# A mixture-of-experts decoder layer: row numbers of a block's last transfer staged and put in place one block later, and the next expert's first weight splits issued ahead of the block counts

## The chip, the cores and the metric

One core of one Trainium2 chip runs the whole program. The metric is device time in microseconds (us), the median of three runs.

## What is computed

The reference is a decoder layer on x of shape (4, 1024, 1024) in float32: causal self-attention with 16 heads, an attention against a context of width 512, and a feed-forward part with 64 experts. Each is added to x. Only the last part, cut to what matters, is touched:

```python
logits = x @ gate_weight.T                       # 4096 tokens, 64 experts
top_val, top_idx = lax.top_k(softmax(logits), 8) # top_val divided by its sum
rerouted = mapping[top_idx]                      # some experts stand in for others
...
gate, up = split(ragged_dot(x[tok], gate_up_proj.T, group_sizes))   # 1024 -> 2 x 384
y = ragged_dot(silu(gate) * up, down_proj.T, group_sizes)           # 384 -> 1024
out = zeros_like(x).at[tok].add(y * w[:, None])
```

How many tokens an expert has is known only at run time.

## The kernel before

The program has four stages: self-attention, mixing with the context, routing, and the experts, from about 3720 us to the end at 7836 us. Only the function `experts` changes.

**Precision.** A float32 product is made of three float32r products: each operand is split into a rounded part (`_hi`) and a rest (`_lo`). ScalarE (ACT in the profile) writes the rounded part with an activation, VectorE (DVE) subtracts it to get the rest, and TensorE (PE) multiplies hi*hi, lo*hi and hi*lo (L1946 to L1948).

**The loop.** All engines run the same loop, `for_experts` (before: L1805 to L1815), over 64 experts. For each expert a `super_block` handles 4 x 128 tokens with the expert's weights. If the expert has more tokens, a counted number of `tail_block`s follows, 64 tokens each, with the same weights. How many there are is the difference of two counts, which each engine reads from SBUF into its registers (`tails_before`, a TENSOR_LOAD, L1803). In `for_experts`, a function `first` may run at the head of an expert, ahead of these two reads; before the change only VectorE has one (`first_weights`, L2333).

**Weights.** An expert has 9 chunks of 512 KB: 0 to 5 for gate and up, 6 to 8 for down. SyncE (SP) loads them into a ring of three slots of `raw_w`; chunk c + 3 is loaded once the rest of chunk c has been made. ScalarE's `split(c)` (L2123) writes `gu_hi` from `raw_w` (L2134), in two halves; VectorE's `rest_of(e, c)` writes `gu_lo` (L2331). TensorE's first layer of an expert waits for the first half of chunk 0's rest.

**Blocks and their last transfer.** A block's results are added to `out` in HBM by indirect transfers that GpSimd (POOL) issues: three for the first three groups of a super block (`send_super`), and for its last group, as for a tail block's only one, two transfers of 64 rows each from `y_last` (`send_last`, L1901, then `send_second`, L1908). These two belong to block n but are issued in block n + 1: ScalarE's `finish_last(n)` (L2114) scales TensorE's result into `y_last` with `w_last`, and the two transfers take their row numbers from `scatter_l` and `scatter_m`. Both transfers raise `yl_sent`; the second waits for the first to land.

The row numbers for the next last transfer may be written into `scatter_l` and `scatter_m` only when the two transfers of this block have landed. VectorE waits for that and copies them: in the middle of a super block (L2378 to L2381), and as the last thing in a tail block (L2424 to L2427).

**The end of a tail block.** TensorE's order is: first layer for the third of the hidden width (f = 2), transpose of f = 1, transpose of the next rows (`turn_tail`, L1982), second layer f = 0, transpose of f = 2, second layer f = 1 and f = 2 (L1954, L1955). ScalarE and VectorE split f = 2's transposed activations (`split_h(2)`, L2195; `rest_of_h(2)`, L2405), which f = 2's second layer waits for, and then the rows that `turn_tail` transposed (`split_tail`, L2104; `rest_of_tail`, L2298).

Of the kernel before, what the change touches and what calls it, by code (L numbers as in the profile page):

```python
# [20 lines left out]
I32 = mybir.dt.int32  # L21
# [5 lines left out]
P = 128  # L27
# [8 lines left out]
FB = F // P  # L36
# [4 lines left out]
START = 1  # L41
# [39 lines left out]
def stand_alone(eng, passed):  # L81


    eng.sem_inc(passed, 1)
# [1634 lines left out]
def experts(nc, const, logits, lo16, hi16, starts, w_gu, w_down, rows, out):  # L1719
# [14 lines left out]
    with ExitStack() as scope:  # L1734
# [29 lines left out]
        scatter_l = m.sb("scatter_l", [P, 1], I32)  # L1764
        scatter_m = m.sb("scatter_m", [T, 1], I32)
        table = m.sb("table", [P, 1 + TAILS + SUP * (E + AHEAD) + LISTED], I32)
        own = m.sb("own", [P, 1])
# [15 lines left out]
        set_up = m.sem("set_up")  # L1783
        mask_ok, list_a, list_ps, list_id, found_ok, list_ok = (
            m.sem(n) for n in ("mask_ok", "list_a", "list_ps", "list_id", "found_ok", "list_ok"))

# [303 lines left out]
        def _(act):  # L2090
# [27 lines left out]
            for i in range(SUP):  # L2118
                split_super(0, i)

            def super_block(e, t0, t1):
                def split(c):

                    act.wait_ge(raw_in[c % RING], START + (e * 3 + c // RING) * 16 + 16)
                    if c < GUC:
                        act.wait_ge(up_ok, START + e * FB)
                        act.wait_ge(tgu_ok, START + t0 * FB)
                        dst = gu_hi[:, c // 2, c % 2 * HALF:(c % 2 + 1) * HALF]
                    else:
                        act.wait_ge(yl_ps, START + (e + t0) * 2 + 2)  # L2130
                        dst = dn_hi[:, c - GUC, :]
                    for q in range(2):
                        a = slice(q * BANK, (q + 1) * BANK)
                        act.activation(dst[:, a], raw_w[:, c % RING, a], ACT.Copy).then_inc(hi_ok, 1)  # L2134

                def silu_of(f):
# [20 lines left out]

                split(0)
                split(1)
                finish_last(e + t0)  # L2160
                split(2)
                split(3)
                silu_of(0)
                split_h(0)
                split(4)
                split(5)
                silu_of(1)
                split_h(1)
                for c in range(GUC, CHUNKS):
                    split(c)  # L2170
                split_tail(e + t0, t0)
# [7 lines left out]
            def tail_block(e, t):  # L2179
# [24 lines left out]
                silu_of(2)  # L2204
                split_h(1)
                split_h(2)
                split_tail(e + 1 + t, t + 1)

            for_experts(act, super_block, tail_block)
            finish_last(E + tails_before(act, E))  # L2210

        @block.vector
        def _(dve):
# [4 lines left out]
            dve.memset(act_t[:, :, :], 0.0).then_inc(set_up, 1)  # L2218
            dve.memset(w_now[:, :], 0.0).then_inc(set_up, 1)
            dve.memset(w_last[:, :], 0.0).then_inc(wl_ok, 1)  # L2220
            dve.wait_ge(set_up, START + 15)
            stand_alone(dve, sl_ok)

# [28 lines left out]
            def finish_list(n):  # L2252
                dve.wait_ge(list_ps, START + n + 1)
                dve.tensor_reduce(found[:, 0, :], ps_l[:, 0:2 * N].rearrange("p (a h) -> p h a", a=2), AX.X, ALU.add).then_inc(list_id, 1)
                dve.wait_ge(list_id, START + n + 1)

                dve.scalar_tensor_tensor(out=found[:, 1, :], in0=found[:, 0, :], scalar=0.0, in1=spare[:, :],
                                         op0=ALU.is_equal, op1=ALU.mult).then_inc(found_ok, 1)
                dve.wait_ge(found_ok, START + n * 2 + 1)
# [3 lines left out]
                dve.wait_ge(found_ok, START + n * 2 + 2)  # L2263
# [5 lines left out]
                ins.then_inc(list_ok, 1)  # L2269
                dve.wait_ge(list_ok, START + n + 1)  # L2270

# [61 lines left out]
            def first_weights(e):  # L2333
                rest_of(e, 0)
                rest_of(e, 1)

            def super_block(e, t0, t1):
                def multiply(f):
# [8 lines left out]
                after = e + AHEAD + 1  # L2347

                dve.wait_ge(wn_ok, START + e + 1)
                dve.wait_ge(ys_ok, START + e * 2 * (SUP - 1))  # L2350
# [42 lines left out]
            def tail_block(e, t):  # L2393
# [33 lines left out]
                dve.tensor_copy(scatter_l[:, :], table[:, bass.ds((e + 1) * SUP + t + 1, 1)]).then_inc(sl_ok, 1)  # L2427

            for_experts(dve, super_block, tail_block, first_weights)


# [62 lines left out]
```

## Time and profile before

| | us |
|---|---|
| median of 3 runs (7830.97 to 7846.51) | 7841.66 |
| the profiled execution, its own time | 7837.53 |
| its span in the trace | 7835.7 |
| TensorE busy (91% of the span) | 7127.5 |
| stage of the experts, from the first to the last microsecond | 4116 |
| TensorE busy in it | 3951 |

The span runs from the first to the last instruction. Matmuls overlap in the trace, so busy time of TensorE says how long it was at work and not how well. The "granted clock" is a share of 2.4 GHz; 0.50 is the lower of its two levels, 1.2 GHz.

### The profile page before, as it was taken

How to read it: one execution, taken by the hardware profiler on the slowest of the kernel's cores; microseconds unless marked ns; L12 is line 12 of the kernel's file. 1: busy time of each engine (PE TensorE's matmuls, PEld its weight loads, DVE VectorE, ACT ScalarE, POOL GpSimd, SP SyncE). 2: the span in 40 equal slices, each digit the busy share in tenths (PEclk: the TensorE clock that was granted, in tenths of full speed). 3: DMA queues.
4: the chain of work that ended last, by engine and by line, in shares of the span. 5: the costliest groups of instructions: out<-in, count | busy, mean ns of one | idle time of the engine just before them, and what ended most of it. 6: DMA issues, size and time to landing. Idle time of an engine off the chain costs nothing.

```text
span 7835.7 us, 118818 instructions
## 1 busy us (share of the span) xinstructions
PE 7127.5 (91%) x37096; PEld 5837.9 (75%) x37098; DVE 4307.2 (55%) x7644; ACT 3545.1 (45%) x6655; POOL 1971.3 (25%) x1711
## 2 busy tenths in 40 slices
PE   7998998998995999992999999999999999999998
PEld 5776776776774877872787777888778787788777
DVE  5666666666664444336555555555555554555554
ACT  4676766666674222210344444444344443344343
POOL 1122122113110000000333333333333333333333
PEclk9999999999997999995999999999999999999999
DMA  2111111111112222221565555655555565566555
GB/s 66 47 55 50 44 56 51 44 56 49 47 43 83 68 69 70 85 68 32 155 170 158 154 154 156 173 163 160 156 156 161 158 181 137 155 171 170 158 138 139
DMA packets 306348, 862.93 MB, mean 110 GB/s; under 512 B 43808, under 2 KB 85280, under 8 KB 306080
## 3 DMA queue, kind: packets, MB, share of 16 engines
q0 software_dynamic: 101680, 369.91, 20.0%
q1 hardware_dynamic: 204400, 489.67, 19.5%
q8 instruction: 142, 2.33, 0.1%
q14 instruction: 126, 1.03, 0.0%
HBM read 617.07 MB, written 208.80 MB: 105 GB/s over the span
## 4 chain that ended last, share of the span: by engine, by line
PE 46%; DMA 4%; issue 1%; DVE 1%; ACT 0%; DVEq 0%; POOL 0%; POOLq 0%; ACTq 0%
PE ps_gu L1946 9%; PE ps_gu L1948 9%; PE ps_gu L1947 9%; PE ps_y L1946 5%; PE ps_y L1948 5%; PE ps_y L1947 5%; PE ps_xe L1973 3%; DMA out<-y_last,scatter_l 2%; DMA out<-y_last,scatter_m 2%; PE ps_l L1962 1%; PE ps_xe L1982 1%; DVE gu_lo L2331 0%; ACT y_last L2114 0%; DVE logits L2237 0%; DMA x_rows<-rows,gather_s 0%
## 5 line engine op out<-in xcount | busy, mean ns | idle before, releaser
L1946 PE MATMUL ps_gu<-xs_hi,gu_hi 128*128 128x512 f32 x3072 | 1242.6, 405 | 133.5 <-DVE gu_lo L2331 133.5
L1948 PE MATMUL ps_gu<-xs_hi,gu_lo 128*128 128x512 f32 x3072 | 1229.1, 400 | 0.0
L1947 PE MATMUL ps_gu<-xs_lo,gu_hi 128*128 128x512 f32 x3072 | 1225.9, 399 | 0.0
L1946 PEld LDWEIGHTS ps_gu<-xs_hi,gu_hi 128*128 128x128 f32 x3072 | 592.9, 193 | 271.8 <-DVE gu_lo L2331 147.0
L1923 POOL TENSOR_TENSOR dn_lo<-raw_w,dn_hi 128x512 fp32r<-128x512 f32 x384 | 485.7, 1299 | 921.5 <-ACT dn_hi L2134 921.5
L1948 PEld LDWEIGHTS ps_gu<-xs_hi,gu_lo 128*128 128x128 f32 x3072 | 592.1, 193 | 131.2
L1947 PEld LDWEIGHTS ps_gu<-xs_lo,gu_hi 128*128 128x128 f32 x3072 | 593.0, 193 | 129.1
L461 PE MATMUL ps_qkv<-xt_hi,w_hi 128*128 128x512 f32 x1512 | 639.6, 423 | 37.8 <-ACT proj L614 30.1
L893 DVE TENSOR_TENSOR pt_lo<-ps_t,pt_hi 128x512 fp32r<-128x512 f32 (+3 forms) x768 | 426.9, 556 | 390.6 <-ACT pt_hi L713 375.3
L1946 PE MATMUL ps_y<-dn_hi,hs_hi 128*128 128x512 f32 x1536 | 628.5, 409 | 0.0
L461 PE MATMUL ps_qkv<-xt_lo,w_hi 128*128 128x512 f32 x1512 | 609.2, 403 | 0.0
L644 ACT ACTIVATE probs<-ps_s,neg_max 128x128 f32<-128x128 f32 (+7 forms) x512 | 379.9, 742 | 503.7 <-DVE neg_max L824 502.8
L1948 PE MATMUL ps_y<-dn_hi,hs_lo 128*128 128x512 f32 x1536 | 606.6, 395 | 0.0
L2146 ACT ACTIVATE hs_hi<-act_s 128x512 fp32r<-128x512 f32 x192 | 121.3, 632 | 1071.3 <-DVE act_s L2341 1071.3
L1947 PE MATMUL ps_y<-dn_lo,hs_hi 128*128 128x512 f32 x1536 | 606.0, 395 | 0.0
L461 PE MATMUL ps_qkv<-xt_hi,w_lo 128*128 128x512 f32 x1512 | 606.0, 401 | 0.0
L2291 DVE TENSOR_TENSOR xs_lo<-ps_xe,xs_hi 128x512 fp32r<-128x512 f32 x520 | 334.5, 685 | 478.0 <-ACT xs_hi L2097 478.0
L2331 DVE TENSOR_TENSOR gu_lo<-raw_w,gu_hi 128x512 fp32r<-128x512 f32 x768 | 486.0, 688 | 149.9 <-ACT gu_hi L2134 142.2
L2134 ACT ACTIVATE gu_hi<-raw_w 128x512 fp32r<-128x512 f32 x768 | 426.8, 620 | 304.8 <-DMA raw_w<-w_gu 225.9
L1893 POOL DMA_INDIRECT out<-y_sup,scatter_s x192 | 300.3, 1564 | 1018.5 <-ACT y_sup L2156 995.3
L2341 DVE TENSOR_TENSOR act_s<-ps_gu,act_s 128x512 f32<-128x512 f32 x192 | 132.8, 692 | 630.0 <-PE ps_gu L1948 630.0
L369 POOL TENSOR_TENSOR w_lo<-w_raw,w_hi 128x512 fp32r<-128x512 f32 x192 | 261.7, 1363 | 852.6 <-ACT w_hi L598 852.5
(332 smaller groups left out, 15818.6 us busy)
## 6 DMA issues: line engine op xcount, KB each, us to landing
raw_w<-w_gu SPq DMA_DIRECT2D x384, 512.0 KB, 4.2
raw_w<-w_down SPq DMA_DIRECT2D x192, 512.0 KB, 6.6
w_raw<-wqkv SPq DMA_DIRECT2D x192, 256.0 KB, 2.6
turned<-proj SPq DMA_DIRECT2D x512, 64.0 KB, 2.0
out<-residual SPq DMA_DIRECT2D x36, 512.0 KB, 2.6
attn_out<-out_t POOLq DMA_DIRECT2D x128, 128.0 KB, 2.3
residual<-x SPq DMA_DIRECT2D x32, 512.0 KB, 5.0
stage<-attn_out SPq DMA_DIRECT2D x32, 512.0 KB, 5.6
```

The source lines that it names most:

```text
L369: pool.tensor_tensor(w_lo[:, i // 2, a, :], w_raw[:, i % RAWS, :, :], raw(w_hi[:, i // 2, a, :]), ALU.subtract).then_inc(w_lo_ok, 1)
L461: mm = pe.matmul(out[:, :], ws[:, kind, k, :], xs[:, k, a], start=(n == 0), stop=(n == 3 * HB - 1))
L644: act.activation(probs[g][:, i, 0:keys], ps_s[:, n % 2, 0:keys], ACT.Exp, bias=neg_max[:, n:n + 1], accum_out=row_sum[:, n:n + 1]).then_in ...
L893: dve.tensor_tensor(pt_lo[:, s % 2, off:], ps_t[:, (1 + at) % 2, off:], raw(pt_hi[:, s % 2, off:]), ALU.subtract).then_inc(tile_lo_ok, 1)
L1893: pool.indirect_dma_start(out, bass.IndirectOffsetOnAxis(ap=scatter_s[:, i:i + 1], axis=0), y_sup[:, i % 2, :], None, compute_op=ALU.add). ...
L1923: pool.tensor_tensor(dn_lo[:, f, a], raw_w[:, f, a], raw(dn_hi[:, f, a]), ALU.subtract).then_inc(dn_lo_ok, 1)
L1946: pe.matmul(out, a_hi, w_hi, start=first, stop=False)
L1947: pe.matmul(out, a_hi, w_lo, start=False, stop=False)
L1948: return pe.matmul(out, a_lo, w_hi, start=False, stop=last)
L2134: act.activation(dst[:, a], raw_w[:, c % RING, a], ACT.Copy).then_inc(hi_ok, 1)
L2291: dve.tensor_tensor(xs_lo[:, ks, a], ps_x1[:, c * BANK:(c + 1) * BANK].rearrange("p (k c) -> p k c", c=P), raw(xs_hi[:, ks, a]), ALU.subtr ...
L2331: dve.tensor_tensor(gu_lo[:, c // 2, b], raw_w[:, c % RING, a], raw(gu_hi[:, c // 2, b]), ALU.subtract).then_inc(lo_ok, 1)
```

## The change

- VectorE has a new small tile `scatter_n`. Where it copied the weights of a block's last transfer to `w_last`, it now also copies that transfer's row numbers to `scatter_n`, which waits for no transfer.
- A new function `place_last(n)` waits until the two transfers of the block before have landed and copies `scatter_n` to `scatter_m` and `scatter_l`. It is called early in each block: in a super block behind `first_weights` and the two reads of counts, in a tail block behind `gather_tail_index`, and once behind the loop. The waits and copies at the old places go.
- ScalarE gets a `first_weights` too: its splits of chunks 0 and 1 now come ahead of the two reads of counts. Their wait on `tgu_ok` goes, and the wait on `yl_ps` that the splits of the down chunks had now stands once ahead of them.
- In a tail block, ScalarE does `split_tail` ahead of `split_h(2)`, and VectorE does the copies of weights and `rest_of_tail` ahead of `rest_of_h(2)`.
- The semaphore `list_ok` goes; `found_ok` counts three steps in its place.

The core of the diff:

```diff
+            def first_weights(e):
+                split(e, 0)
+                split(e, 1)
...
-                split(0)
-                split(1)
                 finish_last(e + t0)
-                split(2)
-                split(3)
+                split(e, 2)
+                split(e, 3)
...
                 silu_of(2)
                 split_h(1)
+                split_tail(e + 1 + t, t + 1)
                 split_h(2)
-                split_tail(e + 1 + t, t + 1)
-
-            for_experts(act, super_block, tail_block)
+
+            for_experts(act, super_block, tail_block, first_weights)
...
+            def place_last(n):
+
+
+                dve.wait_ge(yl_sent, LOADED + n * 32)
+                dve.wait_ge(wl_ok, START + n + 1)
+                stand_alone(dve, passed)
+                dve.tensor_copy(scatter_m[:, :], scatter_n[T:P, :])
+                dve.tensor_copy(scatter_l[:, :], scatter_n[:, :]).then_inc(sl_ok, 1)
...
+                place_last(e + t0)
                 dve.wait_ge(wn_ok, START + e + 1)
...
+                dve.wait_ge(ss_ok, START + e + 1)
+                dve.tensor_copy(scatter_n[:, :], scatter_s[:, SUP - 1:SUP])
                 dve.tensor_copy(w_last[:, :], w_now[:, SUP - 1:SUP]).then_inc(wl_ok, 1)
-                dve.wait_ge(yl_sent, LOADED + (e + t0 + 1) * 32)
-                dve.wait_ge(ss_ok, START + e + 1)
-                dve.tensor_copy(scatter_m[:, :], scatter_s[T:P, SUP - 1:SUP])
-                dve.tensor_copy(scatter_l[:, :], scatter_s[:, SUP - 1:SUP]).then_inc(sl_ok, 1)
...
                 gather_tail_index(e + 1 + t, (e + 1) * SUP + t + 1)
+                place_last(e + 1 + t)
...
                 rest_of_h(1)
-                rest_of_h(2)
                 dve.wait_ge(yl_ok, START + (e + 1 + t) * 2 + 2)
                 dve.wait_ge(wtn_ok, START + e + 1 + t)
                 stand_alone(dve, passed)
+                dve.tensor_copy(scatter_n[:, :], table[:, bass.ds((e + 1) * SUP + t + 1, 1)])
                 dve.tensor_copy(w_last[:, :], wt_next[:, :]).then_inc(wl_ok, 1)
                 dve.wait_ge(wl_ok, START + e + t + 3)
                 keep_tail_weights(e + 1 + t, e)
                 rest_of_tail(e + 1 + t)
-                dve.wait_ge(yl_sent, LOADED + (e + t + 2) * 32)
-                stand_alone(dve, passed)
-                dve.tensor_copy(scatter_m[:, :], table[T:P, bass.ds((e + 1) * SUP + t + 1, 1)])
-                dve.tensor_copy(scatter_l[:, :], table[:, bass.ds((e + 1) * SUP + t + 1, 1)]).then_inc(sl_ok, 1)
+                rest_of_h(2)
```

How the instructions move on VectorE, at the end of a tail block. `ht` is the split activation of the tail, `xtail` the split rows, ISA a register or semaphore instruction; the waits stand in brackets. Before:

```order
L2405 TENSOR_TENSOR ht<-ps_h,ht 128x64 [waits th_hi_ok] x2
L2417 ISA
L2418 REGISTER_ALU [waits yl_ok]
L2420 COPY w_last<-wt_next 128x1 [waits wtn_ok]
L2421 REGISTER_ALU
L2309 ISA [waits wl_ok]
L2311 COPY wt_next<-xt_rows 128x1 [waits rows_t]
L2296 REGISTER_ALU
L2298 TENSOR_TENSOR xtail<-ps_xe,xtail 128x4x64 [waits xtail_hi_ok] x2
L2424 ISA
L2426 ISA [waits yl_sent]
L2426 COPY scatter_m<-table 64x1
```

And with the change, from f = 1's rest to f = 2's, line numbers of the changed kernel:

```order
L2416 TENSOR_TENSOR ht<-ps_h,ht 128x64 [waits th_hi_ok]
L2428 ISA
L2429 REGISTER_ALU [waits yl_ok]
L2431 ISA [waits wtn_ok]
L2431 COPY scatter_n<-table 128x1
L2432 COPY w_last<-wt_next 128x1
L2433 REGISTER_ALU
L2312 ISA [waits wl_ok]
L2314 COPY wt_next<-xt_rows 128x1 [waits rows_t]
L2299 REGISTER_ALU
L2301 TENSOR_TENSOR xtail<-ps_xe,xtail 128x4x64 [waits xtail_hi_ok] x2
L2416 TENSOR_TENSOR ht<-ps_h,ht 128x64 [waits th_hi_ok]
```

The rest for f = 2 has moved behind the copies and both subtractions for `xtail`; there is one more copy (`scatter_n`), and the wait for `yl_sent` is gone from this place, so that what follows is the jump to the next block.

On ScalarE, at the head of an expert, before (`starts` holds the counts):

```order
L1807 ISA
L1803 TENSOR_LOAD starts
L1803 ISA x3
L1803 TENSOR_LOAD starts
L1803 ISA x2
L2124 ISA
L2126 REGISTER_ALU [waits raw_in0]
L2127 ISA [waits up_ok]
L2134 ACTIVATE gu_hi<-raw_w 128x512 [waits tgu_ok]
```

And with the change:

```order
L1808 ISA
L2127 REGISTER_ALU [waits raw_in0]
L2133 ACTIVATE gu_hi<-raw_w 128x512 [waits up_ok]
L2133 ACTIVATE gu_hi<-raw_w 128x512
L2133 ACTIVATE gu_hi<-raw_w 128x512 [waits up_ok,raw_in1]
L2133 ACTIVATE gu_hi<-raw_w 128x512
L1804 ISA
L1804 TENSOR_LOAD starts
L1804 ISA x3
```

The four activations of chunks 0 and 1 stand ahead of the reads of counts now. TensorE's own instructions keep their order, and its two reads of counts stay ahead of its first matmul of an expert.

## Rows read from the trace of the kernel before

**Rows 1.** The page: time by engine, and the clock in 40 slices.

```profile
PE 7127.5 (91%) x37096; PEld 5837.9 (75%) x37098; DVE 4307.2 (55%) x7644; ACT 3545.1 (45%) x6655; POOL 1971.3 (25%) x1711
...
PEclk9999999999997999995999999999999999999999
```

**Rows 2.** Chain of waits, stage of the experts: start us, us, what; matmuls of one list per expert.

```profile
3735.70 0.95 PE ps_l L1962 x32
4113.09 0.95 PE ps_l L1962 x32
4168.30 0.95 PE ps_l L1962 x32
4240.40 0.95 PE ps_l L1962 x32
7773.48 0.95 PE ps_l L1962 x32
```

**Rows 3.** Who waited for whom, 3725 to 7836 us, TensorE: us, times, longest.

```profile
PE ps_gu L1946 <- DVE gu_lo L2331: 125.3, 30, 5.4
PE ps_xe L1982 <- DMA xt_rows<-rows,gather_t: 10.7, 9, 1.8
PE ps_h L2064 <- DVE act_t L2401: 5.7, 5, 2.3
```

**Rows 4.** Timeline of TensorE at one return from a tail block to an expert.

```profile
4222.41 0.40 PE L1955 MATMUL ps_y<-dn_lo,ht 128*128 128x512 f32 x1
4226.98 0.79 PE L1946 MATMUL ps_gu<-xs_hi,gu_hi 128*128 128x512 f32 x1 [4.17 <-DVE gu_lo L2331]
```

**Rows 5.** Timeline of VectorE, same place.

```profile
4221.23 0.22 DVE L2405 TENSOR_TENSOR ht<-ps_h,ht 128x64 fp32r<-128x64 f32 x1 [1.30 <-ACT ht L2195]
4221.96 0.15 DVE L2311 COPY wt_next<-xt_rows 128x1 f32 x1 [0.26 <-DVE w_last L2420]
4222.07 0.75 DVE L2298 TENSOR_TENSOR xtail<-ps_xe,xtail 128x256 fp32r<-128x256 f32 x2
4225.44 0.15 DVE L2426 COPY scatter_m<-table 64x1 int32 x1 [2.62 <-DMA out<-y_last,scatter_m]
4226.23 1.29 DVE L2331 TENSOR_TENSOR gu_lo<-raw_w,gu_hi 128x512 fp32r<-128x512 f32 x2 [0.48 <-issue]
```

**Rows 6.** Timeline of ScalarE, same place.

```profile
4220.97 0.22 ACT L2195 ACTIVATE ht<-ps_h 128x64 fp32r<-128x64 f32 x1 [1.30 <-PE ps_h L2064]
4221.09 0.66 ACT L2104 ACTIVATE xtail<-ps_xe 128x256 fp32r<-128x256 f32 x2
4223.07 2.19 ACT L2134 ACTIVATE gu_hi<-raw_w 128x512 fp32r<-128x512 f32 x4 [1.32 <-issue]
```

**Rows 7.** TensorE's sequencer (PEldq), by line: ns min/median/max, first and last start.

```profile
L1814 PEldq ALU_OP  x1: 32/32/32, 4221.5 to 4221.5; - x1
...
L2009 PEldq FUSED_REGOPS  x1: 51/51/51, 4224.1 to 4224.1; - x1
...
L1803 PEldq TENSOR_LOAD <-starts x126: 295/307/810, 3816.9 to 7759.9; - x126
```

**Rows 8.** Windows: us, busy time of PE, PEld, DVE, ACT, POOL; clock, DMA share, GB/s.

```profile
4155.90:4166.90 11.00, 11.00 (x49) 8.99 (x49) 5.74 (x12) 5.36 (x10) 6.15 (x5) 1.00 0.90 232
4212.40:4222.80 10.40, 9.90 (x72) 8.74 (x70) 3.69 (x13) 3.99 (x12) 3.40 (x3) 1.00 0.62 128
4227.00:4231.60 4.60, 4.60 (x11) 3.63 (x12) 3.34 (x8) 0.61 (x2) 2.85 (x3) 0.50 0.60 125
7604.00:7623.70 19.70, 15.23 (x114) 13.68 (x113) 6.65 (x24) 6.99 (x21) 5.32 (x4) 1.00 0.54 110
```

**Rows 9.** Timeline of TensorE, inside a third tail block in a row.

```profile
3809.76 0.33 PE L2064 MATMUL ps_h<-ident,act_t 128*128 128x128 f32 x1 [2.28 <-DVE act_t L2401]
```

**Rows 10.** Who waited for whom, stage of the experts, VectorE, ScalarE.

```profile
DVE scatter_m L2426 <- DMA out<-y_last,scatter_m: 91.9, 35, 3.9
ACT gu_hi L2134 <- issue: 78.1, 63, 1.8
```

More of the change, by code:

```diff
@@ L1765, in experts @@
         scatter_m = m.sb("scatter_m", [T, 1], I32)
+        scatter_n = m.sb("scatter_n", [P, 1], I32)
         table = m.sb("table", [P, 1 + TAILS + SUP * (E + AHEAD) + LISTED], I32)
@@ L1783, in experts @@
         set_up = m.sem("set_up")
-        mask_ok, list_a, list_ps, list_id, found_ok, list_ok = (
-            m.sem(n) for n in ("mask_ok", "list_a", "list_ps", "list_id", "found_ok", "list_ok"))
+        mask_ok, list_a, list_ps, list_id, found_ok = (
+            m.sem(n) for n in ("mask_ok", "list_a", "list_ps", "list_id", "found_ok"))
         gs_ok, xs_ps, xs_hi_ok, xs_lo_ok, wn_ok, wnow_ok = (
@@ L2119, in _, with split @@
                 split_super(0, i)
-            def super_block(e, t0, t1):
[L2122 to L2134, printed above, removed]
+            def split(e, c):
+                act.wait_ge(raw_in[c % RING], START + (e * 3 + c // RING) * 16 + 16)
+                if c < GUC:
+                    act.wait_ge(up_ok, START + e * FB)
+                    dst = gu_hi[:, c // 2, c % 2 * HALF:(c % 2 + 1) * HALF]
+                else:
+                    dst = dn_hi[:, c - GUC, :]
+                for q in range(2):
+                    a = slice(q * BANK, (q + 1) * BANK)
+                    act.activation(dst[:, a], raw_w[:, c % RING, a], ACT.Copy).then_inc(hi_ok, 1)
+            def first_weights(e):
+                split(e, 0)
+                split(e, 1)
+            def super_block(e, t0, t1):
                 def silu_of(f):
@@ L2156, in finish @@
                         act.activation(y_sup[:, i % 2, a], ps_y[:, a], ACT.Copy, scale=w_now[:, i:i + 1]).then_inc(ys_ok, 1)
-                split(0)
-                split(1)
                 finish_last(e + t0)
-                split(2)
-                split(3)
+                split(e, 2)
+                split(e, 3)
                 silu_of(0)
                 split_h(0)
-                split(4)
-                split(5)
+                split(e, 4)
+                split(e, 5)
                 silu_of(1)
                 split_h(1)
+                act.wait_ge(yl_ps, START + (e + t0) * 2 + 2)
                 for c in range(GUC, CHUNKS):
-                    split(c)
+                    split(e, c)
                 split_tail(e + t0, t0)
@@ L2219, in _ @@
             dve.memset(w_now[:, :], 0.0).then_inc(set_up, 1)
+            dve.wait_ge(set_up, START + 15)
+            dve.tensor_copy(scatter_n[:, :], scatter_l[:, :])
             dve.memset(w_last[:, :], 0.0).then_inc(wl_ok, 1)
-            dve.wait_ge(set_up, START + 15)
-            stand_alone(dve, sl_ok)
             LIST_PARTS = 4
@@ L2258, in finish_list @@
                                          op0=ALU.is_equal, op1=ALU.mult).then_inc(found_ok, 1)
-                dve.wait_ge(found_ok, START + n * 2 + 1)
+                dve.wait_ge(found_ok, START + n * 3 + 1)
                 at = tails_before(dve, n) + n * SUP
@@ L2262, in finish_list @@
                 dve.tensor_tensor(found[:, 0, SUP:], found[:, 0, SUP:], found[:, 1, SUP:], ALU.add).then_inc(found_ok, 1)
-                dve.wait_ge(found_ok, START + n * 2 + 2)
+                dve.wait_ge(found_ok, START + n * 3 + 2)
                 tails = table[:, bass.ds(at + 1 + SUP, 2 * (N - SUP))].rearrange("p (n a) -> p n a", a=2)
@@ L2268, in finish_list @@
                     ins = dve.tensor_copy(tails[T:P, :, half], rows_of)
-                ins.then_inc(list_ok, 1)
-                dve.wait_ge(list_ok, START + n + 1)
+                ins.then_inc(found_ok, 1)
+                dve.wait_ge(found_ok, START + n * 3 + 3)
             def gather_super_index(n, tails):
@@ L2423, in tail_block @@
                 rest_of_tail(e + 1 + t)
-                dve.wait_ge(yl_sent, LOADED + (e + t + 2) * 32)
-                stand_alone(dve, passed)
-                dve.tensor_copy(scatter_m[:, :], table[T:P, bass.ds((e + 1) * SUP + t + 1, 1)])
-                dve.tensor_copy(scatter_l[:, :], table[:, bass.ds((e + 1) * SUP + t + 1, 1)]).then_inc(sl_ok, 1)
+                rest_of_h(2)
             for_experts(dve, super_block, tail_block, first_weights)
+            place_last(E + tails_before(dve, E))
 def rope_tables():
```

## The prediction

> **What bounds the kernel now.** First the page: TensorE is at work for 91% of the span, and the other engines for little over half or less [rows 1]. So time can come from two things only: TensorE standing still, or TensorE running slowly. The line of the clock shows the second, slices at 7 or 5 tenths among the nines.
>
> Next the chain of waits, for the rhythm of the experts' stage. TensorE makes one list per expert (`ps_l`), so the distance of two such pieces is the time of one expert. From 4113.09 to 4168.30 it is 55.21 us, an expert without a tail block. The next, with one tail block, takes 72.10 us [rows 2]. From the first to the last piece there are 63 experts in 4037.78 us. 63 times 55.21 is 3478.2, so 559.6 us belong to tail blocks. A tail block's own work takes 10.4 us (the second window) [rows 8], and there are 35 of them [rows 10]: 364 us. 195.6 us are left, and they are neither work of a super block nor of a tail block.
>
> Who waited for whom says where most of it is: TensorE waited 125.3 us in 30 places for `gu_lo`, the rest of the next expert's first weights; its other waits come to 10.7 and 5.7 us [rows 3]. Thirty is the number of returns from a tail block to the next expert (the 35 tail blocks follow 30 experts), so an expert that follows another directly has no such stall. The mean is 4.18 us.
>
> The windows show the remainder. Right after such a stall the granted clock is 0.50: 11 matmuls take 4.60 us, while between two experts without a tail 49 take 11.00 us at 1.00, 0.224 us each [rows 8]. Eleven at that pace take 2.5 us, so this return loses 2.1 us more. Over all: 195.6 less 125.3 leaves 70 us, of which some 6 to 16 are the other waits; I take 60 us for what the lower clock costs after the 30 stalls, 2.0 us each.
>
> **What ends the stall.** One return, engine by engine. TensorE's last matmul of the tail starts at 4222.41 and ends at 4222.81, the next starts at 4226.98 [rows 4]. VectorE has finished its subtractions for `xtail` at 4222.82, then stands for 2.62 us until the second of the two transfers has landed, copies the row numbers, jumps, and starts `gu_lo` at 4226.23 [rows 5]. It is this wait for a transfer, 91.9 us in 35 places [rows 10], behind which the first weights are queued. ScalarE is earlier: it starts `gu_hi` at 4223.07, after 1.32 us in which it waited for nothing but its own jump and reads of counts [rows 6]; such gaps come to 78.1 us [rows 10].
>
> **The change, part by part.**
>
> *The wait for the transfer leaves the way.* `place_last` now stands behind `first_weights` on VectorE. Nothing holds VectorE at the end of the tail block but its own work. Its jump costs 0.48 us [rows 5].
>
> *ScalarE's first splits come ahead of the reads.* ScalarE ends f = 2's split at about 4221.2 as before (the transposed rows are there first, and `split_tail`, 0.66 us [rows 6], fits into the 1.30 us for which it waited). Then it needs its jump only. The reads were two loads, each some 0.3 us with register steps around them; taking VectorE's 0.48 us for a jump, `gu_hi` starts near 4221.8, and its first half is there near 4222.4, against 4223.7.
>
> *VectorE's order at the end of the tail.* From the start of `ht` at 4221.23 to the end of `xtail` at 4222.82 it needs 1.6 us [rows 5]. With the row numbers' copy, 0.15 us like its neighbours and its register step, I take 1.8 us. These steps now start after f = 1's rest, near 4219.7, and so end near 4221.5; f = 2's rest starts there, 0.3 us later than before. TensorE's last four matmuls wait for it, but f = 1's were running until about then: 0.15 us later, 30 times, is 4.5 us lost (the bounds: 0, if the copy is hidden, and 0.3 us, so 9 us). VectorE is then free for `gu_lo` at 4222.3, and has it started at 4222.4 and its first half ready at 4223.1 (before, TensorE started 0.75 us after VectorE did [rows 4, 5]).
>
> *What is late next: TensorE's own sequencer.* TensorE has its jump and two reads of counts ahead of an expert's first matmul, and the change doesn't move them. In the trace its sequencer takes the tail loop's end at 4221.5, as soon as f = 2's matmuls are passed on, and the last register step ahead of the first matmul at 4224.1 [rows 7]: 2.6 us, ending 1.35 us behind the last matmul. Between experts without tails this is hidden, since many matmuls are queued. Here only four are. It starts 0.3 us later with the change. The loads take 0.307 us in the median but up to 0.810 us [rows 7], so some returns are longer. I take a stall of 1.6 us, with 1.2 us (nothing delayed, quick loads) and 2.3 us (slow loads) as ends. In place of 125.3 us that makes 48 us, and with the 4.5 us from above the stall term is 125.3 - 48 - 4.5 = 73 us; with the ends it is 52 to 89.
>
> The Trainium skill, "DMA: Bandwidth & Descriptors", section "Latency and other measured facts", puts a floor of about 600 ns under a `tensor_load`. The trace's median is half of that [rows 7] and is what the sum uses; by the page's figure the two loads would make the stall 0.6 us longer, and the gain 18 us smaller.
>
> *The clock.* Will a stall of 1.6 us still bring it down? In the tail blocks that follow one another TensorE stands for 2.28 us once [rows 9] and for others over 1 us, and the window over one such pair, with 4.5 us of idle time in 19.7, shows 1.00 throughout [rows 8]. The stalls behind which it fell were around 4.2 us. Between these the nearest rows are the short ones, so I take it that the clock stays up and the 60 us come back. The ends: 64 if all of it does; and a loss rather than a gain if it falls all the same, since more of the slow stretch then holds work instead of idle time (at most another 1 us each, 30 us).
>
> *The rest of the next expert.* `place_last` in a super block waits for the transfer at 4225.3, when VectorE has just done the four rests of chunks 0 and 1. Behind it are the weights and gather indices and the rests of chunks 2 and 3. TensorE needs these only after two products of 24 matmuls, 11 us [rows 8]: cover enough for a delay of some 0.7 us and for ScalarE, whose `finish_last` still waits for the same transfer. POOL gets its row numbers at the same moment as before, so `send_last`, both gathers and `send_second` keep their times. In an expert without a tail ahead, the transfers are long landed, and `place_last` costs two copies and a few register steps, under 0.7 us in 55.21 in which TensorE doesn't wait. In a tail block it stands ahead of an addition that waits for ScalarE, which waits for the same transfers. Nothing.
>
> *Chunk 3's load* starts when chunk 0's rest is done, now 2.6 us or more earlier. That only helps. Start and end of the program: one copy or wait each, beside other work. Nothing.
>
> **The sum.** 73 + 60 = 133 us. The profiled execution took 7837.5 us, 4 below the median, so it would take 7704.5; against the median, 7708.5 us, say 7708.
>
> **The rivals.**
>
> 1. *The stall shrinks and the clock falls all the same.* For it: the lower clock also shows in other stages, where I have not looked for each cause. Against it: the 1.00 over the window of short stalls [rows 8]. It would give 73 us less or, with more work in the slow stretch, 43: 7769 to 7799 us. The Trainium skill, "TensorE: Matmul & The Clock Gate", section "A second HAM failure mode: psum-queue depth-cycling", says that frequent short idle times between groups of matmuls can make the clock go up and down; by it this rival would hold. The trace's run of short stalls does not agree. In between, if it falls at a third of the returns, the time is about 7735.
> 2. *Nothing is left of the stall,* because the sequencer's steps overlap more than the one place shows. Then 125 + 64 = 189 us go: 7652. Against it stand the 2.6 us [rows 7].
> 3. *The change doesn't do what it says:* ScalarE or VectorE is held by something else at this place, for example a load of the chunk, and the stall stays near 4 us: 7830 to 7850. Nothing in the rows shows it: ScalarE waited there for no transfer [rows 6].
> 4. *Slower.* `place_last` at the head of all 64 super blocks holds VectorE ahead of the indices and the rests of chunks 2 and 3, and POOL's first transfer behind `scatter_l`. If that pushed the rests past TensorE's need, each expert would pay. The cover is 11 us less the 5 or so in which chunks 2 and 3 come through after chunk 0; a delay of more than 6 us decides, and to make the kernel slower than before it must cost over 2.1 us in each of 64 experts. The one wait in `place_last` was at most 3.9 us long [rows 10], and that only behind tails.
>
> **How the numbers follow.** A measurement of this kernel tells 0.2% from no change, 16 us. Forecast with the clock up at nearly all returns, 7690 to 7730: 0.66. The clock falling at some or all, 7730 to 7800: 0.22. No stall left: 0.05. Doing nothing: 0.04. Slower: 0.03. The range 7688 to 7770 leaves out rivals 2, 3 and 4 and the upper half of the first, about 0.18. Faster 0.93, same 0.04, slower 0.03.
>
> **What would show it.** TensorE's wait for `gu_lo` after the start should go from 125.3 to under 50 us, or be put down to its sequencer instead; VectorE's wait for the second transfer at the end of a tail should be gone, with a short one at the head of a super block; the granted clock after a return should be 1.00; the spacing of lists without a tail stays at 55.2, and with one tail goes from 72.1 to about 67.5. I am wrong if that spacing without a tail grows, if TensorE waits for a rest of chunk 2 or 3, or if the clock reads 0.50 after most returns.

## The result, and the profile after

The changed kernel takes 7720.18 us (median of 4 runs, 7715.39 to 7720.78) against 7840.98 us before (4 runs, 7830.97 to 7846.51): 120.8 us less, a ratio of 0.9846 with a 95% interval of 0.9829 to 0.9863. The forecast was 7708 us, 133 us less, in a range of 7688 to 7770. One execution of the kernel before, beside e11 and e12, took 27758 us at a granted clock of 0.63 and is left out of their ratios.

The page of the changed kernel, the same two lines as in [rows 1]:

```profile
PE 7089.7 (92%) x37097; PEld 5804.8 (75%) x37098; DVE 4314.6 (56%) x7746; ACT 3548.5 (46%) x6655; POOL 1954.3 (25%) x1711
...
PEclk9999999999998999996899999999999999999999
```

The span is 7718.8 us. TensorE is at work for 92% of it, and for 38 us less in all; that fits fewer matmuls at the lower clock. The line of the clock shows nothing of that: its low slices (the 13th, 19th and 20th of 193 us each now) lie ahead of the experts' stage and at its start, and so did the two in [rows 1]. What the clock costs behind single stalls is too short for a slice and is read from windows.

The chain of waits, one list of TensorE per expert, as in [rows 2]:

```profile
3745.15 0.95 PE ps_l L1963 x32
...
4113.59 0.95 PE ps_l L1963 x32
4168.80 0.95 PE ps_l L1963 x32
4236.21 0.95 PE ps_l L1963 x32
...
7656.25 0.95 PE ps_l L1963 x32
```

An expert without a tail still takes 55.21 us (4168.80 - 4113.59). With one tail the piece that took 72.10 us takes 67.41 (4236.21 - 4168.80). From the first to the last list it is 3911.1 us against 4037.8: 126.7 us less, and all the gain is here.

Who waited for whom, TensorE, from 3735 us on (behind the start), as in [rows 3], and one row of the same view for its weight loads (PEld), which also wait for `ht`:

```profile
PE ps_gu L1947 <- DVE gu_lo L2334: 44.3, 30, 1.8
PE ps_h L2065 <- DVE act_t L2412: 6.6, 5, 1.6
PE ps_y L1955 <- DVE ht L2416: 5.1, 20, 0.3
PE ps_xe L1983 <- DMA xt_rows<-rows,gather_t: 3.8, 5, 1.4
```

```profile
PEld ps_y L1955 <- DVE ht L2416: 19.7, 31, 0.8
```

The wait for the next expert's first weights went from 125.3 us in 30 places to 44.3, 1.48 us each. A new one is there: `ht`, the rest for f = 2, holds the second layer of the tail. Matmuls overlap in the trace, so the row of the matmuls (5.1 us) shows less of it than that of the weight loads (19.7 us).

One return, engine by engine, as in [rows 4 to 6]. TensorE:

```profile
4288.81 0.39 PE L1955 MATMUL ps_y<-dn_hi,ht 128*128 128x512 f32 x1
4289.04 0.40 PE L1956 MATMUL ps_y<-dn_lo,ht 128*128 128x512 f32 x1
4289.56 0.50 PE L1955 MATMUL ps_y<-dn_hi,ht 128*128 128x512 f32 x1
...
4290.36 0.40 PE L1956 MATMUL ps_y<-dn_lo,ht 128*128 128x512 f32 x1
4292.12 0.49 PE L1947 MATMUL ps_gu<-xs_hi,gu_hi 128*128 128x512 f32 x1 [1.36 <-DVE gu_lo L2334]
```

VectorE:

```profile
4287.62 0.23 DVE L2416 TENSOR_TENSOR ht<-ps_h,ht 128x64 fp32r<-128x64 f32 x1
4288.04 0.15 DVE L2431 COPY scatter_n<-table 128x1 int32 x1 [0.19 <-issue]
4288.11 0.14 DVE L2432 COPY w_last<-wt_next 128x1 f32<-128x1 f32 x1
4288.51 0.15 DVE L2314 COPY wt_next<-xt_rows 128x1 f32 x1 [0.26 <-DVE w_last L2432]
4288.62 0.76 DVE L2301 TENSOR_TENSOR xtail<-ps_xe,xtail 128x256 fp32r<-128x256 f32 x2
4289.29 0.21 DVE L2416 TENSOR_TENSOR ht<-ps_h,ht 128x64 fp32r<-128x64 f32 x1
4289.83 1.30 DVE L2334 TENSOR_TENSOR gu_lo<-raw_w,gu_hi 128x512 fp32r<-128x512 f32 x2 [0.32 <-ACT gu_hi L2133]
```

ScalarE:

```profile
4287.60 0.66 ACT L2105 ACTIVATE xtail<-ps_xe 128x256 fp32r<-128x256 f32 x2
4288.54 0.23 ACT L2198 ACTIVATE ht<-ps_h 128x64 fp32r<-128x64 f32 x1 [0.28 <-PE ps_h L2065]
4289.16 2.19 ACT L2133 ACTIVATE gu_hi<-raw_w 128x512 fp32r<-128x512 f32 x4 [0.40 <-issue]
```

And TensorE's sequencer there, by line, as in [rows 7]:

```profile
L1815 PEldq ALU_OP  x1: 32/32/32, 4289.6 to 4289.6; - x1
...
L2010 PEldq FUSED_REGOPS  x1: 51/51/51, 4292.0 to 4292.0; - x1
```

VectorE no longer waits for a transfer at the tail's end. It starts `gu_lo` at 4289.83, before TensorE has finished the tail (4290.76), and ScalarE's gap before `gu_hi` is 0.40 us where it was 1.32. TensorE could have gone on at 4290.5 as far as its data go. Its sequencer came out of the tail's loop at 4289.6 and passed the last register step ahead of the first matmul at 4292.0, and the matmul starts at 4292.12. The view puts the stall down to `gu_lo`, but its first half was done near 4290.5, 1.6 us earlier; the time of the sequencer's last step is what it ends with.

Windows of two returns, from the first matmul of the expert on (span, then busy time and count of PE, PEld, DVE, ACT and POOL, then the granted clock, 1.00 and 0.87):

```profile
4292.10:4303.10 11.00, 10.98 (x48) 8.94 (x48) 3.54 (x11) 4.06 (x7) 6.62 (x6) 1.00 0.79 242
4414.60:4427.30 12.70, 12.69 (x49) 10.07 (x49) 3.45 (x10) 4.05 (x7) 8.39 (x7) 0.87 0.87 268
```

The first 48 matmuls take 11.1 us where the clock stays up and 12.7 where it falls. Before, it fell behind all 30 returns (12.4 to 14.0 us); now behind 6.

Who waited for whom, VectorE and ScalarE, as in [rows 10]:

```profile
DVE scatter_m L2346 <- DMA out<-y_last,scatter_m: 44.4, 34, 3.7
ACT gu_hi L2133 <- issue: 12.1, 30, 0.4
```

The wait for the second transfer is 44.4 us where it was 91.9, and stands at the head of the next block now, where TensorE has two products of 24 matmuls to do with chunks 0 and 1.

### The profile page after: what moved, and what is told of

Read it like the earlier page. It is cut to its first block, busy times and chain, and to the rows that moved or that the text cites. A ratio compares the mean times of both kernels' runs of the same rounds, so it can differ in the third digit from the quotient of the medians.

```text
span 7718.8 us, 118797 instructions
## 1 busy us (share of the span) xinstructions
PE 7089.7 (92%) x37097; PEld 5804.8 (75%) x37098; DVE 4314.6 (56%) x7746; ACT 3548.5 (46%) x6655; POOL 1954.3 (25%) x1711
## 3 DMA queue, kind: packets, MB, share of 16 engines
q1 hardware_dynamic: 204400, 489.67, 19.7%
## 4 chain that ended last, share of the span: by engine, by line
PE 49%; DMA 1%; issue 1%; DVE 1%; ACT 0%; POOL 0%; DVEq 0%; ACTq 0%; POOLq 0%
PE ps_gu L1947 9%; PE ps_gu L1949 9%; PE ps_gu L1948 9%; PE ps_y L1947 5%; PE ps_y L1949 5%; PE ps_y L1948 5%; PE ps_xe L1974 3%; PE ps_xe L1983 1%; PE ps_gu L1955 1%; PE ps_gu L1956 1%; PE ps_l L1963 1%; DVE gu_lo L2334 1%; DMA xt_rows<-rows,gather_t 0%; DMA out<-y_last,scatter_l 0%; ACT gu_hi L2133 0%
## 5 line engine op out<-in xcount | busy, mean ns | idle before, releaser
L1947 PE MATMUL ps_gu<-xs_hi,gu_hi 128*128 128x512 f32 x3072 | 1223.9, 398 | 52.5 <-DVE gu_lo L2334 52.5
L1949 PE MATMUL ps_gu<-xs_hi,gu_lo 128*128 128x512 f32 x3072 | 1207.4, 393 | 0.0
L1948 PE MATMUL ps_gu<-xs_lo,gu_hi 128*128 128x512 f32 x3072 | 1205.0, 392 | 0.0
```

Of the source, the lines that this page charges most:

```text
L1947: pe.matmul(out, a_hi, w_hi, start=first, stop=False)
L1948: pe.matmul(out, a_hi, w_lo, start=False, stop=False)
L1949: return pe.matmul(out, a_lo, w_hi, start=False, stop=last)
```

## The experiments

Times are medians of 4 executions (10 for e2 and e3, 5 for e11 and e12, one for e9 and e10), ratios are against executions of the kernel before beside them, and the kernels of different groups did not run beside each other. "Stall" is the mean time between the end of a tail block's last matmul and the first matmul of the next expert, over the 30 returns; "falls" counts the returns whose first 48 matmuls took over 11.5 us.

### Each part alone

**e1: VectorE's part.** ScalarE's splits and both orders of the tail block are those of before:

```diff
+                split(e, 0)
+                split(e, 1)
                 finish_last(e + t0)
...
-                split_tail(e + 1 + t, t + 1)
                 split_h(2)
+                split_tail(e + 1 + t, t + 1)
...
-            for_experts(act, super_block, tail_block, first_weights)
+            for_experts(act, super_block, tail_block)
...
                 rest_of_h(1)
+                rest_of_h(2)
...
                 rest_of_tail(e + 1 + t)
-                rest_of_h(2)
```

> Only VectorE's part: row numbers staged and put in place in the next block. ScalarE's first splits stand behind its two reads of counts again, and the order at a tail block's end is that of before. My theory (the wait for the transfer made the stall, and TensorE's own jump and two reads of counts are what is left): gu_hi starts some 0.3 us after TensorE's last matmul of the tail as it did before, its rest starts 0.7 us later and TensorE another 0.7 us later, so the stall is 1.6 to 1.8 us against 1.5 with the whole change, f = 2's second layer is not held (5 us less), and the time is 7720 to 7735 us. Rival (ScalarE's early splits carry a good part): stall over 2.5 us, clock down at most returns, 7770 us or more.

Measured: 7715.44 us (7712.07 to 7718.86), ratio 0.9844 (0.9828 to 0.9860), 5 us below the range given. Stall 1.73 us, 7 falls. Its row for the wait at the return:

```profile
PE ps_gu L1947 <- DVE gu_lo L2336: 51.8, 30, 2.0
```

This alone gains as much as the whole change, so the staging of the row numbers is the part that counts. It doesn't make ScalarE's early splits worth nothing: e4 below is this kernel with them, and takes 23 us less beside it (stall 1.46 us, 2 falls). In the whole change the new order takes as much back. What ends the stall is another thing here, too. VectorE waits for ScalarE's `gu_hi`, which comes behind ScalarE's reads, and starts `gu_lo` 0.98 us after the tail's last matmul in the mean; TensorE follows 0.75 us later. At one return:

```profile
4286.51 2.50 DVE L2336 TENSOR_TENSOR gu_lo<-raw_w,gu_hi 128x512 fp32r<-128x512 f32 x4 [0.64 <-ACT gu_hi L2133]
```

**e2: the rest without the staging.** VectorE waits for the transfers and copies the row numbers where it did before; ScalarE's early splits and both new orders stay:

```diff
-                place_last(e + t0)
...
-                place_last(e + 1 + t)
...
                 rest_of_tail(e + 1 + t)
                 rest_of_h(2)
+                dve.wait_ge(yl_sent, LOADED + (e + t + 2) * 32)
+                stand_alone(dve, passed)
+                dve.tensor_copy(scatter_m[:, :], table[T:P, bass.ds((e + 1) * SUP + t + 1, 1)])
+                dve.tensor_copy(scatter_l[:, :], table[:, bass.ds((e + 1) * SUP + t + 1, 1)]).then_inc(sl_ok, 1)
```

> Only the other part: ScalarE's first splits ahead of the reads and the new order at a tail block's end; VectorE waits for the transfer at the end of the tail block and copies the row numbers there, as before. My theory: the stall stays near 4 us, since it ends with the transfer: 7830 to 7845 us, no change. Rival: ScalarE's 1.3 us come off each of 30 stalls: about 7800 us.

Measured: 7839.27 us, ratio 1.0003 (0.9994 to 1.0013), stall 3.94 us, 30 falls. No change, as expected:

```profile
PE ps_gu L1947 <- DVE gu_lo L2334: 118.1, 30, 5.5
```

**e3: the whole change and the wait alone.**

```diff
                 rest_of_tail(e + 1 + t)
                 rest_of_h(2)
+                dve.wait_ge(yl_sent, LOADED + (e + t + 2) * 32)
+                stand_alone(dve, passed)
```

> The whole change, and one wait put back: VectorE waits for the transfer at the end of a tail block, without copying anything there. My theory: TensorE's wait for gu_lo is 110 to 125 us again, the clock is at 0.50 after the stalls, and the time is 7820 to 7840 us. Rival (the copies, the order and the reads matter too): halfway back or less, 7780 us.

Measured: 7833.11 us, ratio 0.9991 (0.9981 to 1.0000), stall 3.47 us, 27 falls.

```profile
PE ps_gu L1947 <- DVE gu_lo L2334: 104.1, 30, 5.1
```

VectorE's own row says what it stands for at the returns:

```profile
DVE gu_lo L2334 <- DMA out<-y_last,scatter_m: 119.6, 30, 5.7
```

One wait brings back nearly all of the time. The stall is 0.5 us shorter than in e2, whose two copies stand behind the wait; 104.1 us is a little under the 110 I gave. That the wait is the cause is shown by this kernel against the change: nothing else differs but the semaphore step behind it (`stand_alone`).

### The order at a tail block's end

**e4: the old order on both engines, with all the rest of the change.**

```diff
                 split_h(1)
-                split_tail(e + 1 + t, t + 1)
                 split_h(2)
+                split_tail(e + 1 + t, t + 1)
...
                 rest_of_h(1)
+                rest_of_h(2)
...
                 rest_of_tail(e + 1 + t)
-                rest_of_h(2)
```

> The whole change with the old order at a tail block's end (the rest for f = 2 ahead of the copies and of the rows' rest on VectorE, the same on ScalarE). My theory: TensorE's 5 us of waiting for ht go, VectorE is free 0.5 us later but still ahead of TensorE's sequencer, so the stall stays 1.4 to 1.6 us: 7710 to 7720 us. Rival (the new order is needed so that VectorE comes to gu_lo in time): stall above 2 us and time above 7740 us.

Measured: 7692.77 us (7689.00 to 7696.78), ratio 0.9812 (0.9796 to 0.9828). That is 27 us less than the whole change (24 us from the first to the last list, means of two traces each), where I had expected 5. TensorE's waits, and the end of one tail block:

```profile
PE ps_gu L1947 <- DVE gu_lo L2334: 43.9, 30, 1.8
PE ps_h L2065 <- DVE act_t L2412: 4.5, 5, 1.6
PE ps_gu L1955 <- DVE xtail L2301: 2.1, 5, 0.4
```

```profile
4284.74 0.39 PE L1956 MATMUL ps_y<-dn_lo,ht 128*128 128x512 f32 x1
4284.97 0.40 PE L1955 MATMUL ps_y<-dn_hi,ht 128*128 128x512 f32 x1
...
4285.67 0.40 PE L1956 MATMUL ps_y<-dn_lo,ht 128*128 128x512 f32 x1
4287.55 0.49 PE L1947 MATMUL ps_gu<-xs_hi,gu_hi 128*128 128x512 f32 x1 [1.48 <-DVE gu_lo L2334]
```

The wait for `ht` is gone, and the matmuls of f = 1 and f = 2 follow each other at 0.23 us. In the changed kernel there are 0.52 us between them (4289.04 and 4289.56). The stall is 1.46 us, as in the change, but there are only 2 falls.

**e7: the old order on VectorE alone.** The last two hunks of e4.

> The whole change with the old order on VectorE alone; ScalarE keeps split_tail ahead of split_h(2). Theory (the 27 us between the change and e4 come from VectorE's copies ahead of the rest for f = 2, which hold TensorE's last four matmuls): 7690 to 7700 us, as e4, and no wait of TensorE for ht. Rival (ScalarE's order does it): 7710 to 7720 us.

Measured: 7694.01 us, ratio 0.9819 (0.9803 to 0.9835), stall 1.51 us, 1 fall, no wait for `ht`; the row of the return:

```profile
PE ps_gu L1947 <- DVE gu_lo L2334: 45.2, 30, 1.8
```

So it is VectorE's order, and ScalarE's makes no difference.

### What is left of the stall

**e5: TensorE's first product ahead of its reads of counts,** on the whole change:

```diff
+            def first_product(e):
+                first_layer(e, 0, 0)
...
-                        pe.wait_ge(tprod_ok, START + t0 * FB)
...
-                first_layer(0, 0)
...
-            for_experts(pe, super_block, tail_block)
+            for_experts(pe, super_block, tail_block, first_product)
```

> The whole change, and on TensorE the first product of an expert (24 matmuls) ahead of its two reads of counts; its wait on tprod_ok goes (TensorE has waited for the same count in the tail block). Theory (the stall that is left, 1.48 us in 30 places, is TensorE's own sequencer): VectorE starts the first rest 0.96 us ahead of the end of the tail's last matmul, and TensorE can start 0.72 us after it, so the stall falls under 0.4 us, and the time by 33 to 50 us with the clock: 7670 to 7690 us. Rival (the first rest or ScalarE sets it): stall stays above 1.2 us, 7715 us or more.

Measured: 7660.52 us (7657.31 to 7665.64), ratio 0.9777 (0.9761 to 0.9794). All of TensorE's waits of over 0.2 us from 3735 us on:

```profile
PE ps_h L2065 <- DVE act_t L2412: 6.9, 5, 1.9
PE ps_y L1955 <- DVE ht L2416: 5.2, 21, 0.3
PE ps_xe L1983 <- DMA xt_rows<-rows,gather_t: 2.4, 3, 1.4
PE ps_gu L1947 <- issue: 0.5, 1, 0.5
PE ps_gu L1947 <- DVE gu_lo L2334: 0.4, 2, 0.2
```

The stall is gone: the next expert's first matmul starts 0.13 us ahead of the modelled end of the tail's last one, as it does between experts without a tail, and there are no falls. The 1.48 us were TensorE's own reads of counts, with the register steps around them. This is 60 us less than the change (61 from the first to the last list, means of two traces each), of which the stalls are 48 (1.61 us in 30 places) and the falls that no longer come, 7 in the mean at 1.6 us, are 11. It is 10 us better than my range, and the fastest version of this study.

**e6: the same on e4** (old order).

> Run e4 (old order at the tail's end) and TensorE's first product ahead of its reads of counts. In e4 VectorE starts the first rest 0.14 us after the tail's last matmul has ended, so TensorE could start at 0.86 us in place of 1.46: 18 us less than e4 and some 3 us of clock, 7668 to 7680 us. Rival (the sequencer isn't the bound in e4): 7690 us or more.

Measured: 7675.17 us (7673.78 to 7678.14), ratio 0.9796 (0.9780 to 0.9813), stall 0.89 us, no falls.

```profile
PE ps_gu L1947 <- DVE gu_lo L2334: 26.6, 30, 0.9
```

From e4's trace 0.86 us had been worked out ahead (0.14 + 0.72). The new order, which costs 27 us in the change, gains 15 us here (e5 against e6): with TensorE's reads out of the way, VectorE sets the start, and in the new order it is there 1.1 us earlier.

**e11: e5 with VectorE's three small copies behind both rests.**

```diff
                 rest_of_h(1)
+                rest_of_tail(e + 1 + t)
+                rest_of_h(2)
                 dve.wait_ge(yl_ok, START + (e + 1 + t) * 2 + 2)
...
                 keep_tail_weights(e + 1 + t, e)
-                rest_of_tail(e + 1 + t)
-                rest_of_h(2)
```

> Run e5 (the whole change, TensorE's first product ahead of its reads) with VectorE's three small copies (row numbers, two of weights) behind both rests at a tail block's end. Theory: the hold of the last four matmuls, some 0.5 us in each of 35 tail blocks, goes, since the copies made it and not the rows' rest; VectorE comes to the first rest about 0.6 us ahead of the tail's end, so the stall is 0 to 0.3 us: 7645 to 7657 us. Rival (the rows' rest itself holds f = 2, whatever the copies do): TensorE still waits for ht, 7660 us or more.

Measured, in five rounds: 7671.69 us (7667.25 to 7674.62), ratio 0.9786 (0.9772 to 0.9800), 13 us above e5 beside it. VectorE at one tail's end, and TensorE's wait:

```profile
4279.87 0.23 DVE L2416 TENSOR_TENSOR ht<-ps_h,ht 128x64 fp32r<-128x64 f32 x1
4280.27 0.76 DVE L2301 TENSOR_TENSOR xtail<-ps_xe,xtail 128x256 fp32r<-128x256 f32 x2 [0.17 <-ACT xtail L2105]
4281.06 0.22 DVE L2416 TENSOR_TENSOR ht<-ps_h,ht 128x64 fp32r<-128x64 f32 x1
4281.38 0.15 DVE L2433 COPY scatter_n<-table 128x1 int32 x1
```

```profile
PE ps_gu L1947 <- DVE gu_lo L2334: 19.4, 30, 0.7
```

The time lies 15 us above the range given, so the theory is half right. TensorE waits for `ht` nowhere, so the copies made the hold, and not the rows' rest. But VectorE comes to `gu_lo` 0.10 us ahead of the tail's end in the mean, not 0.6, because its copies and its jump (0.5 us) are now the last of its work, and the stall is 0.65 us. The stall of 30 times 0.65 us costs more than the hold had.

**e12: e5's kernel again,** beside e11.

> Run e5 again, beside e11 on the same chip, for their difference: 7655 to 7668 us.

Measured, in five rounds: 7658.77 us (7653.40 to 7661.35), ratio 0.9770 (0.9756 to 0.9784), 2 us from e5.

### The clock

**e8: e4 with one more instruction at the end of each tail block on VectorE.** It sums the identity, and nobody reads the sum:

```diff
                 rest_of_tail(e + 1 + t)
+                dve.wait_ge(idle_ok, START + t)
+                dve.tensor_reduce(idle_out[:, :], ident[:, :].unsqueeze(1).broadcast_to([P, 8, P]), AX.X, ALU.add).then_inc(idle_ok, 1)
```

> Run e4 with one more instruction on VectorE at the end of a tail block, a sum over 1024 elements of the identity that nobody reads, about 1.1 us: the stall grows from 1.46 to about 2.2 us. Measures the clock between stalls of 1.5 us (it fell in 2 of 30) and 3.5 us (27 of 30). Theory that the clock follows the length of the stall: it falls in 8 to 20 of 30, and the time is 22 us for the stall plus 10 to 35 us for the clock above e4, 7725 to 7750 us. Rival (only stalls near 4 us bring it down): under 4 of 30 and 7710 to 7720 us.

Measured: 7731.58 us (7728.63 to 7732.08), ratio 0.9867 (0.9850 to 0.9883), 39 us above e4. The stall is 1.96 us, 0.50 more than in e4, and the clock falls behind 11 returns.

```profile
PE ps_gu L1949 <- DVE gu_lo L2336: 58.9, 30, 2.0
```

The stall alone accounts for 15 us, less than the 22 given, and the falls for 15 (11 less 2, at 1.6 to 1.7 us each). Together they are 30; from the first to the last list the two traces differ by 33 us (3922.4 and 3889.5). The two kernels did not run beside each other, so the other 6 us of the 39 say nothing about the edit. The stalls here are all of 1.95 to 1.98 us, and still the clock fell behind 11 and not behind 19. In e6, at 0.89 us, it never fell; in e4 and e7, at 1.5, behind 2 and 1; in e1, at 1.73, behind 7; in e3, at 3.47, behind 27; in e2 and before, at 3.9 and more, behind all 30.

### How far traces of one kernel differ

**e9 and e10: the kernel before and the changed kernel, once more,** one execution each: 7841.81 us and 7726.29 us, with the kernel before at 7826.16 us beside them.

> The kernel before, unchanged, for a second trace. In its first trace the experts' first matmul starts at 3722.7 us; in all the changed kernels' traces between 3726.9 and 3732.5, though the stages ahead are the same code. If that is scatter from one execution to the next, it starts here between 3724 and 3733; if the change moves the earlier stages (placement of the program or of data), it starts at 3722 to 3724 again. From the first to the last list: 4030 to 4040 us either way.

> The changed kernel, unchanged, for a second trace. Scatter: the experts' first matmul starts at 3722 to 3733 us, not at 3732.1 again. From the first to the last list: 3905 to 3920 us; the clock falls after 3 to 10 of the 30 returns, not the same ones, if its falls depend on when the return comes.

The kernel before started its experts 7 us later than in its first trace, with the same code ahead of it:

```profile
3729.89 0.79 PE L1946 MATMUL ps_gu<-xs_hi,gu_hi 128*128 128x512 f32 x1 [8.22 <-DVE gu_lo L2331]
```

In the changed kernel it was 3730.6 us after 3732.1. In the first trace of the kernel before it was 3722.7 us, and in the thirteen others that this study has it lies between 3724.8 and 3732.5: the first one was the early one. From the first to the last list the second traces show 4034.5 and 3918.3 us. In the mean of two traces each, 4036.1 - 3914.7 = 121.4 us were gained there, close to the difference of the medians, 120.8. In e10 the clock fell behind 8 returns, 2 of them the same as in the first trace; in e9 again behind all 30.

## Why the prediction was right

The direction, the place, the mechanism and the range held, and the cause is shown by e1, e2 and e3. The signs named ahead came: the wait for `gu_lo` fell under 50 us, the spacing without a tail stayed, with one tail it came to 67.41 us for "about 67.5", and TensorE waited for no rest of chunk 2 or 3. Term by term, against the first pair of traces (from list to list, 126.7 us less):

| step | predicted | measured |
|---|---|---|
| what is left of the stall, per return | 1.6 us (1.2 to 2.3) | 1.48 us |
| the stall's term, without the hold | 77 us less | 81 us less |
| later rest for f = 2 (the hold) | 4.5 us more (0 to 9) | about 15 us more |
| the clock | 60 us less (a gain of 64 to a loss of 30) | about 52 us less |
| TensorE's other waits | not counted | 7 us less (10.7 + 5.7 + 1.4 before, 3.8 + 6.6 after) |
| sum | 133 us less | 125 of 126.7 us less |

That the sum came within 12 us of the measured time (7708 and 7720) is in part luck: the hold and the clock together gave some 18 us less than forecast, and 11 us of that were made up by a stall that is a little shorter and by other waits of TensorE that nobody had counted.

**The stall.** That the transfer's wait was what it ended with, and that TensorE's own jump and its two reads would be late next, was read from the trace and held: e5 takes these reads out of the way, and the rest of the stall goes. The loads of 0.307 us in the median [rows 7] gave 1.6 us for what is left, and 1.48 was measured. The Trainium skill, "DMA: Bandwidth & Descriptors", section "Latency and other measured facts", has a floor of about 600 ns for a `tensor_load`; by it the stall would have been 2.2 us, an estimate (1.6 + 0.6), and the trace does not agree.

**The hold** is the step that failed, "0.15 us later, 30 times", with 0.3 us as its upper end: it measured 0.4 us, and in the 35 tail blocks, not at the 30 returns alone. I took the time of VectorE's chain right: 1.8 us from f = 1's rest to f = 2's rest was expected, 1.67 us is what it took (4287.62 to 4289.29). What I had wrong is when f = 2's rest is wanted. I read that at one return, at 4221.23, and there TensorE had waited 0.50 us for the gathered rows just before; that waiting had pushed its transpose of f = 2 back. Of 35 tail blocks only 9 have such a wait [rows 3]. In the changed kernel TensorE still waits for these rows in 5, and only there is the hold gone (4 of them) or under 0.1 us (one). In the others ScalarE has f = 2's half ready at once (here at 4288.77), VectorE comes 0.5 us later (4289.29), and TensorE has nothing queued in its place. The tail block that I had read shows no hold after the change either. Measured, it is 24 us from list to list between the change and e4 and e7 (3914.7 against 3890.3 us, means of two traces each), of which about 9 are the falls of the clock that it adds (7 in the mean less 1.5, at 1.6 to 1.7), and some 15 the hold: the second layer of a tail block takes 3.59 us in place of 3.16 in the mean of 35.

**The clock.** "I take it that the clock stays up" was right for 24 and 22 of 30 returns. That the clock was low among the experts was read from the windows; the slices at 7 and 5 tenths in [rows 1], which the prediction also names for it, lie ahead of that stage. The rows behind "stays up", a stall of 2.28 us and a window with several stalls at 1.00, were no proof for 30 places: e8 shows that a stall of 1.96 us brings the clock down at a third of them. Part of the falls comes from the hold, since e4 has the same stall and 2 falls. So the two misses are mostly one: without the hold the time is that of e4, 7693 us, 15 below the forecast.

Rival 1, the clock down at most or all returns, did not come, but a part of it did: 6 and 8 of 30, where I had taken none into the sum. The Trainium skill, "TensorE: Matmul & The Clock Gate", section "A second HAM failure mode: psum-queue depth-cycling", says that frequent short idle times between groups of matmuls can make the clock go up and down. The traces agree with it in part: behind stalls of about 1.5 us the clock fell at 6 and 8 of 30 returns, behind those of 0.89 us (e6) at none. One window at 1.00 was too little to set it aside for all.

**The rivals.** Rival 2 (no stall left) is refuted by the trace, and e5 shows what it would have taken. Rival 3 (the stall stays near 4 us) is refuted by the 1.48 us of the trace. Rival 4 is refuted by the spacing of 55.21 us, unchanged. `place_last` at the head of a block costs nothing that any trace here shows.

## What to carry to other kernels

When a wait is taken off the path, look at the sequencer of the engine that was waiting: jumps and register loads that were hidden behind the wait can be the next bound, and work that does not need the loaded values can be issued ahead of them (60 us here, half as much as the change itself). Read the slack of a moved instruction at several places, and first look whether the place chosen has a wait of its own that the others lack; a gain on one engine's order may be paid on another (e4 against e6). And take small parts of a change singly: of the three here the staging won 125 us (e1), ScalarE's early splits 23 more (e4), and the new order cost 27 of these 148.

## What was not expected of the hardware

- The clock's falls do not follow from the stall's length by a sharp bound: 11 of 30 stalls of equal length, 1.95 to 1.98 us, brought it down, and which of the returns it was differed between two executions of one kernel (e10). Behind stalls of about 1.5 us, an extra hold of 0.3 to 0.5 us in the tail block's second layer, some 1.2 us ahead of the stall, raised the falls from 2 and 1 (e4, e7) to 6 and 8 (the change, e10).
- Where it fell, 48 matmuls took 12.7 us in place of 11.1: 1.6 us. Behind the long stalls of before it was 2.0 us in the mean: over these 48 matmuls the granted clock was 0.79 to 0.83 at 16 of 30 returns, where behind the short stalls it was 0.87.
- The stages ahead of the experts, with the same code in all 14 traces, ended up to 10 us apart (3722.7 to 3732.5 us), more than some of the terms above, so small terms are compared between lists and not between spans.
